# Seven down-weight halves ahead of the attention, own buffers for one LN2 tile, and paced weight loads

## The reference

```python
x = x + attn(layernorm(x))            # one head of width 256, softmax over 2048 keys
x = x + ffn(layernorm(x))             # as below
# ffn(h):
rw, _ = top_k(h @ gate_w, 2)          # 8 experts, sum of the two best logits
h2 = relu(h @ up_w) ** 2              # 1024 -> 2048
shared = h2 @ down_w                  # 2048 -> 1024
moe = (h @ fc1_w) @ expert_w * rw.sum(-1)
return layernorm(shared + moe @ fc2_w) * ln_gamma + ln_beta
```

## Time and profile before

| | us |
|---|---|
| median of 3 runs (2358.00 to 2361.13) | 2360.07 |
| the profiled execution's own time | 2361.47 |
| its span, first to last instruction | 2359.7 |
| PE busy in the span (98%) | 2318.3 |
| weight loads on PE (82%) | 1945.5 |
| DVE busy (67%) | 1576.2 |
| ACT busy (33%) | 788.8 |
| POOL busy (12%) | 291.8 |

### The profile page before, as it was taken

The page is one execution under the profiler, slowest core; times in us unless marked ns, Lnnn a source line. Parts: engine busy times, 40 slices in busy tenths (PEclk is TensorE's granted clock), DMA queues, the critical chain, the costliest instruction groups (busy, mean ns, idle before and its releaser), DMA issues.

```text
span 2359.7 us, 27222 instructions
## 1 busy us (share of the span) xinstructions
PE 2318.3 (98%) x10888; PEld 1945.5 (82%) x10888; DVE 1576.2 (67%) x1758; ACT 788.8 (33%) x875; POOL 291.8 (12%) x574
## 2 busy tenths in 40 slices
PE   9999999989999989999999999999999999999997
PEld 8988988878888878788888888888888888888886
DVE  7777539888998864488774268865238876425447
ACT  4333326657655431421212231213132121223210
POOL 3010000000132300032210013300003221000002
PEclk9999999999999989999999999999999999999999
DMA  8999524545434688879996678898668899666865
GB/s 302 337 359 363 207 64 148 171 139 201 160 118 164 241 271 301 320 265 312 325 336 212 191 247 290 329 331 279 190 222 271 308 335 322 209 195 205 241 205 179
DMA packets 232831, 581.86 MB, mean 247 GB/s; under 512 B 25984, under 2 KB 79872, under 8 KB 232320
## 3 DMA queue, kind: packets, MB, share of 16 engines
q1 hardware_dynamic: 151328, 444.57, 57.2%
q10 hardware_dynamic: 81376, 135.55, 15.6%
HBM read 424.58 MB, written 155.45 MB: 246 GB/s over the span
## 4 chain that ended last, share of the span: by engine, by line
PE 81%; DVE 7%; DMA 7%; ACT 3%; issue 1%; POOL 1%; SPq 0%; ACTq 0%; DVEq 0%; POOLq 0%
PE psum L114 80%; DMA wu_s<-QR0a 2%; DMA QR0a<-in_upfc_dram 1%; DMA wd_s<-QRc 1%; DVE mx L102 1%; PE psum L353 1%; ACT SA L99 1%; DVE QR0a L102 1%; DVE HB L102 1%; DVE QRc L102 1%; DMA att_s<-ATT 1%; DVE acc L102 1%; ACT ATT L99 1%; DVE st L188 1%; DMA WR<-wu_s 1%
## 5 line engine op out<-in xcount | busy, mean ns | idle before, releaser
L102 DVE TENSOR_TENSOR HB<-HB,psum 128x1024 f32<-128x1024 f32 x140 | 169.1, 1218 | 287.1 <-PE psum L114 287.1
L99 ACT ACTIVATE HB<-HB 128x1024 f32<-128x1024 f32 x128 | 135.7, 1061 | 342.9 <-DVE HB L102 340.9
L105 POOL TENSOR_SCALAR veA<-mvA 128x1 f32<-128x1 f32 x32 | 31.0, 970 | 1302.1 <-DVE mvA L191 1302.1
L114 PE MATMUL psum<-XS1h,WR 128*128 128x512 f32 x560 | 177.3, 394 | 6.5 <-DMA WR<-wu_s 5.4
L114 PE MATMUL psum<-XS2h,WR 128*128 128x512 f32 x560 | 176.4, 394 | 3.4 <-DVE XS2l L102 3.4
L114 PE MATMUL psum<-XS0h,WR 128*128 128x512 f32 x560 | 175.5, 390 | 0.0
L114 PE MATMUL psum<-XS3h,WR 128*128 128x512 f32 x560 | 174.1, 389 | 0.0
L114 PEld LDWEIGHTS psum<-XS1h,WR 128*128 128x128 f32 x560 | 106.3, 190 | 30.2 <-DMA WR<-wu_s 6.6
L114 PEld LDWEIGHTS psum<-XS2h,WR 128*128 128x128 f32 x560 | 106.5, 190 | 26.1 <-DVE XS2l L102 3.8
L114 PEld LDWEIGHTS psum<-XS3h,WR 128*128 128x128 f32 x560 | 105.1, 188 | 21.8
L114 PEld LDWEIGHTS psum<-XS0h,WR 128*128 128x128 f32 x560 | 105.1, 188 | 21.7
(11 more groups left out here) (310 smaller groups left out, 5880.0 us busy)
## 6 DMA issues: line engine op xcount, KB each, us to landing
WR<-wu_s SPq DMA_DIRECT2D x280, 512.0 KB, 4.3
WR<-wd_s SPq DMA_DIRECT2D x280, 512.0 KB, 4.8
att_s<-ATT ACTq DMA_DIRECT2D x32, 516.0 KB, 3.4
RAW<-in_x_dram SPq DMA_DIRECT2D x32, 512.0 KB, 8.6
RES<-x1b_s SPq DMA_DIRECT2D x128, 128.0 KB, 5.5
wd_s<-QHc ACTq DMA_DIRECT2D x18, 896.0 KB, 4.7
wd_s<-QRc ACTq DMA_DIRECT2D x18, 896.0 KB, 4.4
HB<-xT_s SPq DMA_DIRECT2D x14, 1024.0 KB, 8.3
```

Of the source, the lines that this page charges most:

```text
L99: return act.put(lambda e: e.activation(o, i, f, **kw), *toks)
L102: return (q or dve).put(lambda e: e.tensor_tensor(o, a, b, op=op), *toks)
L105: return (q or dve).put(lambda e: e.tensor_scalar(o, a, s1, s2, op0=op0, op1=op1), *toks)
L114: return pe.put(lambda e: e.matmul(o, w, m, start=start, stop=stop, **kw), *toks, sig=sig)
```

## The change

- Seven of the twelve halves leave the attention. They are done in steps 68 to 91 of the QKV loop and inside the eight score steps (names "S0" to "S7", run behind `mx_op(0, k)`): four through a new buffer QD that lies where `RAW[0]` lay (free after the last even x tile), three through QE, where `XA[0]`'s low part lay. Each buffer's next load waits for the stores of its half before. The first halves that remain in the attention are at steps 0, 3, 6, 9 and 12.
- What is laid over QD and QE later (mx, KVR, QR, the P buffers) now waits for their last stores.
- The fourth LN2 tile of token group 1 (tokens 512 to 1023) gets buffers of its own, `XL[3]`, starts at chunk 7 instead of 8 and its steps stand closer; its stores stand at chunk 9 instead of 11, `x_load` at 11 instead of 12, the sums and the pieces of T2 one chunk earlier in part.
- The first weight loads into slots 1, 2 and 3 wait for pieces 4, 8 and 11 of the last but one output projection, and that into slot 4 also for `pv_t[7,0]`.

No arithmetic is added or taken away.

```diff
@@ mx_op
-            mx_t[i, k] = TT(mx[:, :], SA[:, sa(i, 0), :], s, ALU.max, S_ev[i, 0], S_ev[i, 1])
+            mx_t[i, k] = TT(mx[:, :], SA[:, sa(i, 0), :], s, ALU.max, S_ev[i, 0], S_ev[i, 1], *(() if i else quad_st["qd"]))
@@ QKV plan
+    QD, QE = ((at(f"QR{n}", [128, 8, 256], F32, o), at(f"QH{n}", [128, 7, 256], F32R, o + 8), None)
+              for n, o in (("d", 176.5), ("e", 128.5)))
...
+    for m, (buf, name, steps) in enumerate((
+            (QD, "qd", (68, 70, 71, 72, 72, 72, 73)), (QD, "qd", (74, 76, 77, 78, 78, 78, 79)),
+            (QD, "qd", (80, 82, 83, 84, 84, 84, 85)), (QD, "qd", (86, 87, 88, 89, 89, 89, 90)),
+            (QE, "qe", (84, 86, 87, 88, 88, 88, 89)), (QE, "qe", (90, 91, "S0", "S1", "S1", "S1", "S2")),
+            (QE, "qe", ("S3", "S4", "S5", "S6", "S6", "S6", "S7")))):
...
+                plan.run(f"S{k}")
@@ weight loads
-    w_first = {0: lambda: (S_pe[7, 7],), 4: lambda: chain(6, 7), 5: lambda: (pv_t[7, 6],)}
+    w_first = {0: lambda: (S_pe[7, 7],), 1: lambda: (wo_pe[6, 4],), 2: lambda: (wo_pe[6, 8],), 3: lambda: (wo_pe[6, 11],),
+               4: lambda: (*chain(6, 7), pv_t[7, 0]), 5: lambda: (pv_t[7, 6],)}
@@ attention plan
-    for m in range(12):
-        plan.add(3 * m, dn_half, plan, m, (3 * m + 1, 3 * m + 2, 3 * m + 2, 3 * m + 2), lambda m=m: quad_st["qc"] if m else t2_first)
-    plan.add(36, lambda: [task() for task in late] and late.clear())
+    for m in range(5):
+        plan.add(3 * m, dn_half, plan, 7 + m, (3 * m + 1, 3 * m + 2, 3 * m + 2, 3 * m + 2), lambda m=m: quad_st["qc"] if m else t2_first)
+    plan.add(15, lambda: [task() for task in late] and late.clear())
@@ seam
-                    ln2_at(plan, 4 * tt - 4, LN2_U0[tt - 1], 1, tt, LX, LA, BO, T2, (BETA_A, ld_beta_a), (1, tt - 1))
+                    lx, la, p = (*XL[3][:2], None) if tt == 3 else (LX, LA, (1, tt - 1))
+                    free = dict(lx_free=(pv_t[7, 7],), la_free=(pv_t[7, 7],)) if tt == 3 else {}
+                    ln2_at(plan, c, LN2_U0[tt - 1], 1, tt, lx, la, BO, T2, (BETA_A, ld_beta_a), p, **free)
+                plan.add((0, 4, 7)[tt - 1], run)
-                plan.add(12, x_load, 0, 1, r, lambda: (pv_t[7, 7],))
+                plan.add(11, x_load, 0, 1, r, lambda: (pv_t[7, 7],))
-                plan.add(14 + n // 2, x_sum, s, name, h)
+                plan.add((13, 14, 15, 17)[n // 2], x_sum, s, name, h)
-                plan.add(16 + h, x_piece, s, "T2", h)
+                plan.add(16, x_piece, s, "T2", h)
```

More of the change, by code:

```diff
@@ L717, in transformer_layer, with run @@
             plan.add(b + 2 * a, lambda u=u, a=a, n=b + 2 * a + 1: plan.at.setdefault(n, []).insert(0, xt_evac(u, a)))
+    for m, (buf, name, steps) in enumerate((
[3 more added lines that the diff above has]
+            (QE, "qe", ("S3", "S4", "S5", "S6", "S6", "S6", "S7")))):
+        def run(m=m, buf=buf, name=name, steps=steps):
+            free = quad_st.get(name, (xt_pe[6, 3],) if name == "qd" else (t_pv[6, 3],))
+            tasks = quad_tasks("d", 1 + m // 2, *buf, name, 256, m % 2, *free)
+            tasks[0]()
+            for n, task in zip(steps[1:], tasks[1:]):
+                plan.add(n, task)
+        plan.add(steps[0], run)
     for j, w in enumerate("kv"):
@@ L766, in transformer_layer @@
     T2 = at("T2", [128, 4, 8, 4, 32], F32, 204.71875)
-    stg = {"n": 0, "free": {0: (xt_pe[7, 3],), 1: (xt_pe[7, 3],)}, "bufs": [KVR[:, 0, :], KVR[:, 1, :]], "pre": "kvr"}
+    stg = {"n": 0, "free": {n: (xt_pe[7, 3], *quad_st["qd"]) for n in range(2)}, "bufs": [KVR[:, 0, :], KVR[:, 1, :]], "pre": "kvr"}
     ld_bo = [dma(BO[:, :], bo.rearrange("(a n) -> a n", a=1).to_broadcast([128, 1024]), "bo", xt_pe[7, 3])]
@@ L818, in pfree @@
         n = 8 * i + k - 3
-        return (pv_t[n // 8, n % 8],) if n >= 0 else (t_A,)
+        return (pv_t[n // 8, n % 8],) if n >= 0 else (t_A, *quad_st["qe"])
     def P_h(i, k):
@@ L1074, in x_piece @@
         elif name == "T3":
-            toks += [dn_pe[s - 1, 3, 9] if s else pv_t[7, 7]]
+            toks += [dn_pe[s - 1, 3, 9]] if s else [ln2_tr[1, 3], x1b_st[1, 3], gl_t[1, 3]]
         else:
```

7 lines of the change are left out of this document (3 added, 4 removed).

## The result

| | before | after |
|---|---|---|
| median, us | 2359.98 (13 runs, 2357.1 to 2362.98) | 2364.61 (13 runs, 2359.99 to 2369.45) |
| the profiled execution's own time | 2361.47 | 2360.72 |
| its span | 2359.7 | 2358.9 |
| mean granted clock | 0.994 | 0.995 |

The ratio of after to before is 1.0019, 95% interval 1.0011 to 1.0028: 4.6 us slower where I had said 16 us faster. A second measurement of the same kernel gave 1.0010 (1.0001 to 1.0019). The forecast of 2344 and its range, 2336 to 2353, missed. The profiled execution of after lies 3.9 us under its own median, while that of before lies above: the two profiles alone show a tie.

A forecast was written before the change was run, and what follows sets the result against it. PE was taken as the bound, with only its lost time to win. Profiled 2361.47, less 8.3, 13.1 and 1.0, plus 6.2, made 2345.3; less 1.4 for profile over median, 2343.9, called 2344 us, range 2336 to 2353.

The forecast's parts named there:

- halves out of block 2: End of attention block 2: removing the halves there ends PE's 4.14 us wait and what follows it, gaining 8.3 us.
- halves into the QKV stage: End of the QKV stage: free up to step 83, then a chain costing 6.2 us, bounds 0 and 10.
- seam: Stretch 840 to 880 us: earlier fourth LN2 tile removes the waits at chunks 18 and 20, gaining 13.1 us.
- pacing: First weight loads held back: shorter PE waits for ATT near 764 and 769 us, gaining 1.0 us, between 0 and 1.4.
- the walk from step 84: QKV stage's end: stores, loads, sums and splits followed link by link, putting PE's transposes 4.4 us later, at 346.0.
- the slide of ACT's evacuations: QKV stage: ACT's evacuation of 310.19 slides behind a half's `high`, called harmless since its bank is wanted at 316.5.
- the 4.0 and 3.6 that I named: Each link of the QKV stage's chain: low part's store lands 4.0 us after issue, next load 3.6 later.
- the stretched chain: Slower rival, steps 84 to S7: stores landing in 9.5 us delay the transposes by 22, giving 2366; chance 0.06.
- The wait that I had forecast, for mx: Behind the first v product, QKV stage's end: PE waits 3.5 to 4.5 us for mx, then a low clock.
- stores and load back keep their lengths: In the 840 to 880 us stretch's chain: xT's stores still take 11.27 us and HB's load 6.19, only shifted earlier.
- the margins of 2.8 and 0.8 us: Chunks 18 and 20: weights and T2's second low part ready 2.8 and 0.8 us before PE wants them.
- a wait costs clock when it is over 3 us: PE throughout: a wait over 3 us brings the low clock and costs some 2.5 us more; shorter ones don't.

The follow-up runs named there:

- the kernel with three halves: Kernel before, with three halves instead of seven in the QKV stage and nine in attention: 2354.37 us, ratio 0.9962; repeated, 2356.80 us, 0.9971.
- the kernels with five and four halves: Changed kernel without paced weight loads, five or four halves in the QKV stage, the others back in attention: 2358.01 us (0.9979) and 2350.88 us (0.9951).
- the kernel with XS1r late: Three halves in the QKV stage, LN2 tile buffers and paced weight loads as changed, XS1r loaded after the last output-projection piece: 2354.03 us, ratio 0.9962.
- the kernel with three halves, the seam and pacing: Changed kernel with three halves instead of seven in the QKV stage and nine in attention: 2351.00 us, ratio 0.9956.
- the second profile of after: The changed kernel measured once more, nothing altered: 2365.62 us, ratio 1.0010; its profiled execution took 2361.23 us.

## Why the prediction was wrong

| part | forecast, us | two profiles | measured by runs |
|---|---|---|---|
| halves out of block 2 | -8.3 | -9.2 | -7 to -9 |
| halves into the QKV stage | +6.2 | +13.4 | +14 to +16 |
| both | -2.1 | +4.2 | +6.9 |
| seam | -13.1 | -7.0 | -5.0 |
| pacing | -1.0 | +2.2 | 0 to +3 |

In the last column the first row is the kernel with three halves (0.9962, 0.9971), which loses nothing in the QKV stage, and the second is the 6.9 of both less that. 6.9 less 5.0 and up to 3 makes 2 to 5 us; measured were 4.6 and 2.4. The middle column (+4.2 - 7.0 + 2.2) makes -0.6; the two profiled executions differ by -0.75.

**Block 2: right.** 8.3 said, 9.2 found, and no wait for mx near 512.

**The halves in the QKV stage: the chain was forecast, its length and its longest wait were not.** The step that failed is the walk from step 84. It had the low parts, stores and loads in the right order, but took their landing from a stretch with one half on the way, and it put the slide of ACT's evacuations at nothing. Its links in the chain of after:

```profile
303.49 7.01 DMA wd_s<-QRd
...
310.99 3.69 DMA QRd<-in_dn_dram
...
318.30 4.16 DMA wd_s<-QRe
...
322.95 7.79 DMA QRe<-in_dn_dram
...
338.41 4.12 DMA wd_s<-QRe
...
343.00 3.12 DMA QRe<-in_dn_dram
```

From the issue of a store to the landing of the load behind it my walk has 7.7, 8.3 and 7.7 us, 23.7 in three (the 4.0 and 3.6 that I named make 22.8; the walk is looser than its own terms by 0.9). They took 11.2, 12.4 and 7.7, 31.3: 7.6 more. The first store was issued at 303.49 instead of 300.6, 2.9 later, and the work between the links took 0.9 less. That makes the 9.6 by which the transposes were later than I said (355.6 for 346.0). The 4.0 came from the attention, where one half is on the way at a time. Here two buffers and the key, value and q transfers are. Their landing in the changed kernel, 255 to 350 us (KB each, median us):

```profile
wd_s<-QHd ACTq DMA_DIRECT2D x4, 896.0 KB, 5.6
wd_s<-QRd ACTq DMA_DIRECT2D x4, 896.0 KB, 5.8
```

The worst is a load: QRe, 7.79 us for 256 KB each, issued at 322.5 after ACT had issued three stores at 318.3, 318.7 and 320.7, 2.7 MB together. Last in the chain, with no store of a half on the way, the same load took 3.12. The Trainium skill, "DMA: Bandwidth & Descriptors", section "Queues, rings and completion order", says that each DMA engine takes turns between the queues that have work for it, a packet at a time. The trace agrees in that a load on SP's queue took 2.5 times as long beside stores on ACT's (7.79 against 3.12); without the stores of the halves these loads took 3.0 us in the median, with them 4.7. The order of packets no row shows. My argument against the stretched chain, that the stretch is among the emptiest for DMA, read a share (0.21) from before that the change itself made 0.67. Without the stores it was 0.29. From 300 to 310 us, where the chain's first store stands, the share was 0.53 even before, and 0.99 after.

A second fault stands in the same walk. I called the slide of the evacuation of 310.19 harmless and left out the one behind it, which has no slack at all: before the change PE already waited 0.87 us for OUT at its first score product:

```profile
316.46 0.47 PE L114 MATMUL psum<-Q0h,KH 128*128 128x512 f32 x1 [0.87 <-ACT OUT L99]
```

Its place on ACT after the change:

```profile
316.30 1.79 ACT L99 ACTIVATE QHd<-QRd 128x1024 fp32r<-128x1024 f32 x2 [4.50 <-DVE QRd L102]
317.99 0.67 ACT L99 ACTIVATE OUT<-psum,bqs 128x512 f32<-128x512 f32 x1
318.30 0.38 ACTq L95 DMA_DIRECT2D wd_s<-QRe  x1
318.72 0.58 ACTq L95 DMA_DIRECT2D wd_s<-QHd  x1
319.33 1.33 ACTq L95 DMA_DIRECT2D qk_s<-OUT  x1
320.71 0.63 ACT L99 ACTIVATE Q1h<-STG 128x512 fp32r<-128x512 f32 x1 [2.05 <-DVE QRd L102]
320.74 1.21 ACTq L95 DMA_DIRECT2D wd_s<-QRd  x1
322.05 0.69 ACT L99 ACTIVATE OUT<-psum,bqs 128x512 f32<-128x512 f32 x1 [0.71 <-issue]
```

The first OUT stands behind a `high` whose sums waited for QD's load, the second behind four stores, two of which (QRe and QRd) wait for low parts of DVE. That is the 6.87, for which the sum had nothing, and the kernels with five and four halves show that it is the fourth QD half's. The wait that I had forecast, for mx, came at 3.7 (3.5 to 4.5 said), but the low clock that I put behind it did not. The walk also called that pause, about 4 us, longer than any of the three before; one of them was 4.14. The rival of a stretched chain named the mechanism, but only as 22 us with a chance of 0.06. What came was 13.4 in the trace and 14 to 16 by the runs, above my upper bound of 10 and short of the rival's 22.

**The seam: the term was 13.1 and is 5 to 7.** By its own steps, with the 5.8 us taken off by which all is later: the second add stood at 817.7 where I said 816.3, since its load was issued at 816.8 (816.8 less 5.8 is 811.0) behind a weight load that waited, and took 6.6 us (before, the same load took 4.8). The stores began at 825.6 where I said 824, and the last was issued 4.2 us earlier than before. What failed is "stores and load back keep their lengths": the stores did, the load did not. The chain of after:

```profile
816.79 6.64 DMA XLA<-att_s
...
834.94 10.99 DMA xT_s<-T
845.94 10.29 DMA HB<-xT_s
```

HB took 10.3 in after instead of 6.2, and 9.3 to 10.7 in twelve more profiles with this part (8.6 in the kernel with XS1r late), against 5.7 to 7.5 in the four others without it; 4.1 of the gain went there. Three weight loads are issued in the 8 us ahead of it, which is why I tried half-sized ones, but these brought only 9.1. Before and after, the DMA engines are 0.89 to 0.98 busy in this stretch, and what limits them there stays open. So the margins of 2.8 and 0.8 us were not there, and this is what was left:

```profile
860.26 0.50 PE L114 MATMUL psum<-XS1h,WR 128*128 128x512 f32 x1 [2.38 <-DMA WR<-wu_s]
864.11 0.50 PE L114 MATMUL psum<-XS1h,WR 128*128 128x512 f32 x1 [0.84 <-DMA WR<-wu_s]
871.05 0.47 PE L114 MATMUL psum<-XS2h,WR 128*128 128x512 f32 x1 [1.16 <-ACT SB L99]
```

SB I had not costed: with both pieces of T2 at chunk 16 its copy stands on ACT behind them. The low clock did go, as forecast. Some of the gain comes back behind 900 us, where PE loses 3.4 us on average in the nine profiles that have this part and no edit beyond halves and pacing (2.0 to 6.0) and 1.0 to 2.2 in the five without.

**Pacing: 0 instead of 1.** With and without it the ratios are 0.9956 and 0.9953. That agrees with what the Trainium skill says in "DMA: Bandwidth & Descriptors", "Queues, rings and completion order", that each DMA engine works through a ring in order, which I had set against the pacing; the order itself no row shows. The 2.2 of the middle column is not its cost: profiles without pacing differ by over 6 us among themselves from 700 to 800 us. What 768 to 777 us does show is a cost that I had excluded, a low clock behind a short wait (below).

**Which run is profiled.** I carried before's 1.4 us between profile and median over to after. After's runs spread over 9.5 us, and its profile lay 3.9 below their median. So of the miss of 20.6 us the two profiles show 15.4, and the other 5 come from this step.

## What to carry to other kernels

Before work is moved into a stretch that looks empty, add its own transfers to the stretch: a landing time read where one half is on the way (4.0 us) did not hold where the change put several (up to 7.0, and 7.8 for a load). Work with a store-then-load link may be put where nothing behind it on its engines is wanted at once; look for evacuations and copies that PE already waits for, however briefly (0.87 us here), since these have no slack. And of a change in several parts measure each alone: here the seam was worth 5 us and three of the seven halves 7 to 9, and the other four cost 13 to 16.

## What the runs showed of the hardware

- The length of the wait just before does not tell whether the clock falls. In after it fell behind a single wait of 2.25 us: 1.5 us of work later, at 770.2, and ahead of the next wait. A matmul of 344 columns, 0.16 us from start to start, takes 0.29 from there on, and those of 512 columns 0.43 until 776.94, instead of 0.23:

```profile
768.70 0.42 PE L114 MATMUL psum<-WOH,OH 128*128 128x344 f32 x1 [2.25 <-ACT ATT L99]
...
770.04 0.37 PE L114 MATMUL psum<-WOH,OH 128*128 128x344 f32 x1
770.21 0.49 PE L114 MATMUL psum<-WOL,OH 128*128 128x344 f32 x1
...
772.97 0.77 PE L114 MATMUL psum<-PH,VH 128*128 128x512 f32 x1 [1.69 <-ACT ATT L99]
```

  In the trace of before, waits of 2.23 and 2.10 us at the same place left it at 1.00. In the kernel with three halves, the seam and pacing it is 0.50 from 687.8 on, behind a wait of 1.89 us for mx at 686.4; in the second profile of after a wait of 2.91 us for mx at 701.4 left it at 1.00. And behind the 3.69 us at 355.62 in after it is 1.00 from 355.6 to 362, where the four transposes take 0.66 us together, not the 1.12 of the earlier trace rows. My reading that a wait costs clock when it is over 3 us, and only then, fails on both sides.
- A load of two times 256 KB took 3.1 us with no store of a half on the way, and 7.8 beside 2.7 MB of stores from the other queue; stores of 896 KB in the same chain took 4.1 to 7.0.
- The length of a wait is no measure of the time behind it: in the changed kernel 6.87 us for OUT were followed by eight matmuls in 3.55 us, 1.7 us lost, less than the 2.4 that I had counted behind 4.14 us, and no low clock at all followed the 3.69.
